# Eight-layer sequence kernel: fp4 gates issued two tiles ahead, and the local-attention layer with scaled rotation tables, folded squares and another order

## The reference

```python
# fp4 layer: W_gate, W_up (352, 128), W_down (128, 352)
def fp4_quant_dequant(x):                  # blocks of 16 along the last axis
    scale = jnp.maximum(max(abs(xb)) / 6.0, 1e-12)
    idx = jnp.searchsorted(_MID, jnp.abs(xb / scale))
    return _GRID[idx] * jnp.sign(xb) * scale
fp4_linear = lambda x, w: fp4_quant_dequant(x) @ fp4_quant_dequant(w).T
h = jax.nn.silu(fp4_linear(x, w_gate)) * fp4_linear(x, w_up)
return fp4_linear(h, w_down)               # h is quantised again

# local layer: DEPTH 6, BATCH 4, 1024 tokens, 16 heads of 64, window 32
x = shift_tokens(x) ...                    # half of the features one token back
q, k, v = split(x @ Wqkv, 3)
q = l2norm(q) * q_scale;  k = l2norm(k) * k_scale
q = q * cos * scale + rotate_half(q) * sin * scale
k = k * cos / scale + rotate_half(k) * sin / scale
sim = q . k * 8.0        # each window of 32 against itself and the one before
x = x + softmax(where(mask, -max, sim)) @ v @ Wo
xn = layernorm(x); a, gate = split(xn @ W1 + b1)
x = x + (a * gelu(gate)) @ W2 + b2
```

## Time and profile before

| | us |
|---|---|
| runs | 8266.29, 8272.07, 8274.26 |
| median | 8272.07 |
| profiled execution | 8273.95, with a span of 8272.2 from first to last instruction |
| mean granted clock of TensorE | 0.925 of full |
| busy: PE, DVE, ACT, POOL | 6963.6, 6292.9, 2558.4, 3060.0 |
| fp4 layer, about | 2968 to 3340 |
| entry, and the loop of local | 4445 to 4545, and 4545 to 8215 |

### The profile page before, as it was taken

One profiled execution on the slowest core, in us unless ns is written; L12 is line 12 of the kernel. 1 busy time (PEld: TensorE's weight loads), 2 busy tenths in 40 slices (PEclk: granted clock), 3 DMA queues, 4 the chain that ended last, 5 costly groups with the idle time before them and its releaser, 6 DMA issues. The chain is left out here.

```text
span 8272.2 us, 238749 instructions
## 1 busy us (share of the span) xinstructions
PE 6963.6 (84%) x91001; PEld 4056.2 (49%) x91001; DVE 6292.9 (76%) x14037; ACT 2558.4 (31%) x4951; POOL 3060.0 (37%) x3870
## 2 busy tenths in 40 slices
PE   4999999999975753687875999999999999999997
PEld 3666666666631221253343555555555555555554
DVE  8777777777767566696884787787887888887876
ACT  2111111111133321313213344444444443444444
POOL 0333333333300000030201555555555555555553
PEclk7999999999987866888978999999999999999999
DMA  0000000000000000000003121111211121211111
GB/s 21 1 1 1 0 0 0 1 0 1 0 5 1 4 11 0 0 1 1 1 1 109 53 59 53 56 56 53 59 53 56 56 60 57 59 53 56 56 55 63
DMA packets 156918, 242.42 MB, mean 29 GB/s; under 512 B 21616, under 2 KB 136848, under 8 KB 150160
## 3 DMA queue, kind: packets, MB, share of 16 engines
q1 hardware_dynamic: 155920, 228.45, 9.2%
HBM read 186.66 MB, written 13.66 MB: 24 GB/s over the span
## 5 line engine op out<-in xcount | busy, mean ns | idle before, releaser
L2832 POOL TENSOR_TENSOR big<-big 128x512 f32<-128x512 f32 x388 | 496.2, 1279 | 1769.8 <-DVE big L2670 1709.5
L2842 POOL TENSOR_TENSOR big<-big 128x512 f32<-128x512 f32 x776 | 1081.2, 1424 | 18.7 <-DMA big<-norms 3.9
L834 POOL TENSOR_TENSOR big<-big 128x128 f32<-128x128 f32 x1024 | 415.4, 406 | 1342.3 <-DVE big L780 1341.9
L2234 PE MATMUL banks<-hidden,big 128*128 128x256 f32 x3104 | 812.1, 399 | 73.1 <-DMA hidden<-big 36.2
L600 ACT ACTIVATE banks<-banks 128x128 f32<-128x128 f32 x1024 | 268.3, 262 | 1825.9 <-DVE banks L763 1825.9
L489 PE MATMUL banks<-big 128*128 128x256 f32 x2050 | 733.8, 440 | 62.3 <-ACT big L574 60.0
L2298 PE MATMUL banks<-big,hidden 128*32 128x512 f32 x6144 | 784.5, 603 | 0.0
L1933 POOL TENSOR_TENSOR big<-big 128x448 f32<-128x448 f32 (+10 forms) x160 | 142.5, 891 | 1717.9 <-DVE weights_odd L1797 1645.9
L2277 PE MATMUL banks<-big 32*32 32x64 f32 (+1 forms) x49152 | 637.7, 223 | 135.8 <-issue 135.5
L2234 PEld LDWEIGHTS banks<-hidden,big 128*128 128x128 f32 x3104 | 558.4, 192 | 391.6 <-issue 87.3
L2277 PEld LDWEIGHTS banks<-big 32*32 32x32 f32 x49152 | 524.8, 104 | 405.6 <-issue 405.3
(11 more groups left out here) (358 smaller groups left out, 13818.0 us busy)
## 6 DMA issues: line engine op xcount, KB each, us to landing
big<-norms SPq DMA_DIRECT2D x776, 128.0 KB, 2.9
big<-qk SPq DMA_DIRECT2D x50, 512.0 KB, 4.5
big<-vo SPq DMA_DIRECT2D x25, 1024.0 KB, 5.6
weights_odd<-ffn SPq DMA_DIRECT2D x25, 537.5 KB, 4.4
hidden<-big SPq DMA_DIRECT2D x171, 64.0 KB, 12.9
hidden<-big SPq DMA_DIRECT2D x25, 256.0 KB, 3.0
hidden<-big SPq DMA_DIRECT2D x25, 255.8 KB, 3.7
big<-pairs SPq DMA_DIRECT2D x6, 1024.0 KB, 11.3
```

The source lines that it names most:

```text
L834: nc.gpsimd.tensor_tensor(full(u["kS"][s % 2]), full(S), by(u["ko_c"]), ALU.mult).then_inc(*e.did(("kS", s)))
L2234: mm = self.nc.tensor.matmul(bank[:, n * QTOK:(n + 1) * QTOK], u["w" + name.lower()][:, (2 * g + n) * P:(2 * g + n + 1) * P], u["xs"][:, a ...
L2832: self.nc.gpsimd.tensor_tensor(dst, cos, sin, ALU.add).then_inc(*e.did(("turned_pair", f, name, g)))
L2842: self.nc.gpsimd.tensor_tensor(x, x, u["norms"][:, n, g].unsqueeze(1).broadcast_to([P, 2, QTOK]), ALU.mult).then_inc(*e.did(("scaled", f, ...
```

## The change

In fp4: the gates are made two tiles ahead. VectorE's order becomes gated(0), gated(1), then for each g round(g), down(g-1), gated(g+2), and down(7) at the end; TensorE and ACT follow in the same order (up(0), up(1), then down(g-1), up(g+2); split(g+1), turn(g-1), silu(g+2)). The eight copies into `xq_t` go from VectorE to ACT.

In local:
- `rope` becomes one tensor_tensor of 128x512 and two of 128x256 with tables that hold the scale already. ACT makes these in `table` (eight copies of 128x256 with a scale, each quarter, two sets in turn), from base tables that SP loads anew for each quarter (`base_in`, four transfers of 128 KB). The load of the scales goes from VectorE (L2776) to ACT (`rescale`, f=2). The entry loads two quarters of the base tables instead of all.
- POOL adds the two halves of each square (`fold_squares`, eight of 128x256 a quarter), and `sums` has four calls instead of eight.
- The order is another on TensorE, ACT, VectorE and POOL. attend(f-1,1) stands behind three K projections; of the scores of the first half one stands alone and three together, behind Q's third projection; those of the second half stand four together (f=0,1) or three and one (f=2,3). ACT's exponential of the second half is taken in its own quarter, and VectorE's lowering before it there too; its normalising comes first in the next quarter.

```diff
 def fp4_vector
     gated(0)
+    gated(1)
     for g in range(TILES):
-        if g + 1 < TILES:
-            gated(g + 1)
         dve.wait_ge(*e.after("split", g))
         round_fp4(...)
-        down(g)
+        if g:
+            down(g - 1)
+        if g + 2 < TILES:
+            gated(g + 2)
+    down(TILES - 1)
 def local_sync
         for f in range(QUARTERS):
+            pf, kw = earlier(f)
+            hold(core, e, *e.after("table", pf, "Q", 1, **kw))
+            base_in(core, st, sp, f)
 def sums
-        pe.wait_ge(*e.after("squares", f, name, GROUPS - 1))
-        for n in range(2):
-            for g in range(GROUPS):
-                mm = matmul(bank[...], spread, u["sq"][g][:, n * QTOK:(n + 1) * QTOK], start=n == 0, stop=n == 1)
+        pe.wait_ge(*e.after("folded_squares", f, name, GROUPS - 1))
+        for g in range(GROUPS):
+            mm = matmul(bank[...], spread, u["sq"][g][:, 0:QTOK], start=True, stop=True)
 def local_tensor
             t.project(f, "K", 0)
             t.project(f, "K", 1)
-            t.value(f, 0, 0)
-            t.value(f, 0, 1)
             t.project(f, "K", 2)
+            t.attend((f - 1) % QUARTERS, 1)
             t.project(f, "K", 3)
             t.score_masks(f, 0)
             t.score(f, 0, 0)
+            t.turn_back(f)
...
+            t.sums(f, "K")
+            t.project(f, "Q", 0)
+            t.project(f, "Q", 1)
+            t.project(f, "Q", 2)
             t.score(f, 0, 1)
             t.score(f, 0, 2)
-            t.attend((f - 1) % QUARTERS, 1)
...
             t.score_masks(f, 1)
             t.score(f, 1, 0)
-            t.project(f, "Q", 3)
-            t.value(f, 1, 0)
-            t.sums(f, "Q")
             t.score(f, 1, 1)
...
 def rope
-        stt(part(0), x[0], s[:, 0:1], cos, ALU.mult, ALU.mult)
-        stt(part(1), x[1], s[:, 1:2], cos, ALU.mult, ALU.mult)
-        stt(part(2), x[1], s[:, 2:3], sin, ALU.mult, ALU.mult)
-        stt(part(3), x[0], s[:, 0:1], sin, ALU.mult, ALU.mult)
+        tt(m[:, 0:2 * QTOK], bank, cos, ALU.mult)
+        tt(m[:, 2 * QTOK:3 * QTOK], bank[:, QTOK:2 * QTOK], sin[:, 0:QTOK], ALU.mult)
+        tt(m[:, 3 * QTOK:4 * QTOK], bank[:, 0:QTOK], sin[:, QTOK:2 * QTOK], ALU.mult)
+    def table(self, f, name, j):
+        base = u["base"][2 - 2 * n + j]
+        out = u["table"][(f + 1) % 2][:, n, j, :]
+        for k in range(2):
+            activation(out[:, k * QTOK:(k + 1) * QTOK], base, ACT.Copy, scale=s[:, c:c + 1])
+    def fold_squares(self, f, name, g):
+        self.pool.wait_ge(*e.after("squares", f, name, g))
+        gpsimd.tensor_tensor(sq[:, 0:QTOK], sq[:, 0:QTOK], sq[:, QTOK:2 * QTOK], ALU.add)
 def local_vector
+            v.normalise((f - 1) % QUARTERS, 1)
             v.rope(f, "K", 0)
-            v.normalise((f - 1) % QUARTERS, 1)
...
             v.guard(f, "K")
-            v.lower(f, 0)
+            v.add(...)
             v.rope(f, "Q", 0)
             v.rope(f, "Q", 1)
             v.rope(f, "Q", 2)
+            v.lower(f, 0)
             v.guard(f, "Q")
             v.rope(f, "Q", 3)
             v.normalise(f, 0)
...
+            v.lower(f, 1)
 def local_pool
+            p.fold_squares(f, "K", 0)
+            p.fold_squares(f, "K", 1)
+            p.fold_squares(f, "K", 2)
+            p.fold_squares(f, "K", 3)
             p.add(f, "K", 0)
```

More of the change, by code:

```diff
@@ L1317, in up, with down @@
             core.product(e, core.to_dve, [(u["xq_t"][:, a:a + P], u["up_t"])], cols=HID)
-    up(0)
-    for g in range(TILES):
-        if g + 1 < TILES:
-            up(g + 1)
+    def down(g):
         pe.wait_ge(*e.after("hq", g))
@@ L1331, in fp4_tensor @@
                                       for k, (a, m) in enumerate(KC)])
+    pe.wait_ge(*e.after("wq_used"))
+    up(0)
+    up(1)
+    for g in range(TILES):
+        if g:
+            down(g - 1)
+        if g + 2 < TILES:
+            up(g + 2)
+    down(TILES - 1)
     core.norm_pe(e, "ln", u["y"], u["lnsq"], ("y",))
@@ L1347, in fp4_scalar @@
         core.found.at[("fp4", "x_parts", t)] = core.found.at[("fp4", *label)]
+    for t in range(TILES):
+        bank, label = core.drain(e, core.to_act)
+        nc.scalar.activation(u["xq_t"][:, tok(t)], bank, ACT.Copy).then_inc(*e.did(label))
+        core.found.at[("fp4", "xq_t", t)] = core.found.at[("fp4", *label)]
     def silu(g):
@@ L1357, in silu, with split @@
             core.found.at[("fp4", "silu", g, j)] = core.found.at[("fp4", *label)]
-    silu(0)
-    for g in range(TILES):
-        if g + 1 < TILES:
-            silu(g + 1)
+    def split(g):
         act.wait_ge(*e.after("gated", g, 3))
@@ L1376, in fp4_scalar @@
         core.found.at[("fp4", "h_t", g)] = core.found.at[("fp4", *label)]
+    silu(0)
+    silu(1)
+    split(0)
+    for g in range(TILES):
+        if g + 1 < TILES:
+            split(g + 1)
+        if g:
+            turn(g - 1)
+        if g + 2 < TILES:
+            silu(g + 2)
+    turn(TILES - 1)
     core.norm_act(e, "ln", u["y"], u["lnsq"], ("y",), "eps5")
@@ L1399, in fp4_vector @@
     core.found.at[("fp4", "wq_used")] = core.found.at[("fp4", *label)]
-    for t in range(TILES):
-        bank, label = core.drain(e, core.to_dve)
-        nc.vector.tensor_copy(u["xq_t"][:, tok(t)], bank).then_inc(*e.did(label))
-        core.found.at[("fp4", "xq_t", t)] = core.found.at[("fp4", *label)]
     def gated(g):
@@ L2102, in entry_sync @@
         low.then_inc(*st["xs"].loaded("xs" if q else None))
+    sp.wait_ge(*e.after("table", 2, "Q", 1))
+    base_in(core, st, sp, 3)
     for name, n in (("K", 0), ("Q", 1)):
@@ L2392, in entry_scalar @@
     core.nc.scalar.preload_act_table_set(LN_EXP)
+    e.eng.wait_ge(*e.after("scale"))
+    for name in NAMES:
+        for j in range(2):
+            a.table(2, name, j)
     for name in NAMES:
@@ L2396, in entry_scalar @@
         a.inverse(3, name)
+    for name in NAMES:
+        for j in range(2):
+            a.table(3, name, j)
     for d in range(DEPTH):
@@ L2424, in entry_vector @@
     dve.wait_ge(*e.last())
-    dve.wait_ge(*e.after("tables"))
     for name in NAMES:
@@ L2701, in normalise @@
         p, total = u["prob"][jj], u["total"][jj]
-        dve.wait_ge(*e.after("exp", f, jj))
+        if e.layer == "local":
+            dve.wait_ge(*e.after("exp", f, jj, **({"back": 1} if jj and f == QUARTERS - 1 else {})))
         self.nc.vector.tensor_reduce(total, p, AX, ALU.add).then_inc(*e.did())
@@ L2786, in local_vector @@
             v.guard(f, "K")
-            v.lower(f, 0)
+            v.add(f, (turn % BATCH) * SEQ + (f - 1) * QTOK if f else old + 3 * QTOK)
             v.rope(f, "Q", 0)
```

171 lines of the change are left out of this document (103 added, 68 removed).

## The result

| | before | after |
|---|---|---|
| median of 20 runs, us | 8273.38 | 8287.41 |
| ratio to before, 95% interval | | 1.0018 (1.0011 to 1.0025) |
| profiled execution, us (span) | 8273.95 (8272.2) | 8284.18 (8282.4) |
| first projection of the entry, us | 4481.8 | 4388.4 |
| turn of local, us | 151.8 | 155.9 |

One of the 20 executions of the changed kernel took 11479.77 us, which the median doesn't feel.

A forecast was written before the change was run, and what follows sets the result against it. A handover bounds fp4, TensorE's own program bounds local. A local turn was 137.3 - 3.5 + 14.6 + 4.5 = 152.9 us against 151.8, +26 over 24 turns; 8274 - 88 - 5 + 26 = 8207 us, range 7970 to 8300.

The forecast's parts named there:

- fp4: fp4 layer: gates two tiles ahead remove VectorE's idle at tile boundaries, copies go to ACT; -88 us, from -75 to -92.
- The entry: Entry of local: filled with transfers, 1 MB less of tables to load; -5 us, from -8 to 0.
- The added work: Local: POOL's folds, ACT's table copies and SP's loads are added; all three costed at nothing.
- The issue gaps: Local, long score bursts: seven or eight of eight hold a whole instruction packet; 14.6 us a turn in place of 7.2.
- rival R: Local: issue gaps vanish altogether and both new chains bound, 138 to 140 us a turn, 7860 to 7920 us; chance 0.05.
- The clock: Local: half-clock stretches follow the gaps, 3.1 a turn at 1.45 us; 4.5 us a turn (2.6 to 6.7).
- The 137.3: Local: us a turn of TensorE's own rows at full clock, left from 151.8 after issue gaps, VectorE waits and half-clock losses.
- the third of "what gets shorter": Local: reordered attends and values remove TensorE's waits for VectorE's results; -4.7 us a turn, 0 to 3 may return.
- rival D: Whole kernel: the two (A's and C's slowdowns in local) cancel fp4's gain, 8256 to 8289 us; chance 0.10.
- Rival C: Local: POOL starts the K folds late, +5 to 8 us a turn, 8325 to 8400 us, slower; chance 0.16.

The follow-up runs named there:

- run with 44 products: Changed kernel with 44 additional one-column products in the entry, moving the local loop's code 176 instructions further on: ratio 0.9908 to the kernel before.
- tail: Changed kernel with the last quarter's down product put behind its last three values, so six long products end the loop: ratio 1.0138 to the kernel before.
- tail2: tail with VectorE's normalise(3,1) moved to the end of its own turn, in front of the addition for that down product: ratio 0.9949 to the kernel before.
- split: Changed kernel with a value call put between score products in both halves, same instructions in other places on TensorE only: ratio 0.9967 to the kernel before.
- split2t31: tail2 with scores taken apart another way than in split, plus 31 one-column products in the entry: 8059.59 us, ratio 0.9744 to the kernel before.
- bsplit: Kernel before with the new fp4 stage, and in local two values moved between the first three windows of scores: ratio 0.9845 to the kernel before.
- bphase46: Kernel before with the new fp4 stage and 46 one-column products in the entry, local's loop 184 instructions further on: ratio 0.9884 to the kernel before.

## Why the prediction was wrong

**fp4: right.** -88 forecast, -91.4 measured at its last down add, by the mechanism forecast, with 0.4 us left a tile, the "few tenths".

**The entry: wrong, and small.** -5 forecast. By its first projection another 2.0 us are won, and behind it 6.6 are lost. I had priced its transfers alone; the fold, which I had put at nothing, stands uncovered in front of its two sums and costs 12.6 us of waiting there. That -93 and -93.4 agree is chance: the place where the 93.4 are read lies ahead of that wait.

**The added work: right.** By the two long stretches, a turn has 23.5 us more of POOL (23.6 forecast) and 13.8 more of ACT (13.2), and 9.3 less of VectorE (8.8).

**The issue gaps: right, and the largest term.** 14.6 us a turn forecast; 12.8 before scores and 1.1 before up products measured. Seven gaps a turn, of 1.1 to 2.6 us in the turn shown, stand in or right behind the eight bursts; the one in the first burst of f=3 was forecast and isn't there. The run with 44 products shows that the code's place makes them. The Trainium skill ("Runtime: NRT & Kernel Launch", section "Instruction fetch mechanics") has the block of 256 instructions right and calls its crossing mostly hidden; here it costs up to 2.6 us where the block before is used up in 1.43 us, and the rival R built on that rule is refuted.

**The clock: right in kind.** 4.5 us forecast with the half-clock stretches. TensorE's busy time a turn, which holds its own rows and the slow ones, was to be 137.3 - 3.5 + 4.5 = 138.3 us and was 137.2. Some 0.7 of the difference is the base. The 137.3 wasn't all TensorE's own work: a wait of the variance products for ACT had stayed in it, which is gone after the change. Before, from 4700 to 8000 us:

```profile
PE banks L2345 <- ACT hidden L2573: 14.4, 22, 0.7
```

**The step that failed is the third of "what gets shorter", the -4.7 us of waits.** I had counted the 15.4 us of L2234 behind VectorE's L2763, 1.1 us a turn, as a wait for data that values would cover. It is the jump at the end of the loop, and with 24 short products at the end it costs 2.9 us: +1.8 instead of -1.1. The runs tail and tail2 show it: other products in front of the jump, and the wait is 1.0 us again. And of the attention values' wait 1.6 us stayed, at attend(1,1) in f=2, of which I had put 0 into the sum and 3 into the upper bound only. Together 137.2 + 12.8 + 1.1 + 2.9 + 1.6 + 0.3 of smaller ones = 155.9. The forecast had 152.9. The step alone is 4.8 us a turn too low (2.9 + 1.6 + 0.3, where the sum had nothing left), 115 us; gaps that came out 0.7 smaller and the 1.1 less of TensorE's own time hid some of it by luck. The 3 us a turn that remain are 72 us of the 77 between 8207 and the profiled 8284; the entry has the other 6, and the exit gives 1 back.

**The range and the chances.** The time is inside the range, at its upper end, on the wrong side of no change. My rival D had the outcome (8256 to 8289) at 0.10. I had priced it as the two parts of the change cancelling, without a mechanism of its own; the jump would have been one. Rival C, POOL, wasn't it in the loop of the changed kernel, whose sums don't wait for the fold; only the two of the entry do. In the loop it came true only in split, once the two values in front of the Q sums had gone, and in part in the comparison without the fold.

## What to carry to other kernels

Where an engine runs many short instructions in a row, count its instructions against the pace of its code: a block of them that is used up sooner than the next one arrives stalls the engine, and the profile calls it "issue". Spread short instructions among long ones, put long ones at the end of a loop, and try the same loop some dozens of instructions further on, since an order's gain or loss of 1% can hang on that alone. A wait that occurs exactly once in a turn, at the first product after the jump, may be the jump's, whatever releaser the profile infers; here it was. Count what the probe itself costs: 64 one-column products took 25 us. And before a gap is closed, ask which handovers it covers: here each of the three ways of taking the scores apart (split, split2t31, bsplit) uncovered a wait for another engine.

## What the hardware showed that was not expected

The jump back in TensorE's loop costs about 1 us behind six long products (2.84 us, 12 instructions with their weight loads) and 2.8 to 3.0 us in the mean behind 24 short ones (2.85 us, 48 instructions): the same time, another number of instructions. So the jump seems to be taken up a certain number of instructions ahead and not a certain time ahead; some 3.9 us for the jump and 16 instructions ahead would give both. This is an estimate from these two cases and wasn't tested by itself. It isn't the whole of it: in bphase46 six long products end the loop as in the kernel before, only the code's place is another, and the jump costs 1.7 us and not 1.1.

The half-clock stretches stand behind waits for data as well as behind issue gaps. Before and after, 21 of 34 and 68 of 118 gaps of about 2 us and more in the scores were followed by a half-clock stretch. In split2t31, 35 of the 36 stretches stand behind waits for data: 19 behind 2.3 to 3.5 us for VectorE's normalise, 16 behind 1.9 us for kept values. Without the fold the normalise waits are down to 1.8 us, and although the scores have more gaps (125 against 110, none over 1.8 us) five stretches are left, 0.2 a turn in place of 1.6.
